# Queries and keys projected with rows on partitions, and brought to their stacks through a scratch array

## What is computed

```python
q = (target @ Wq.T + bq).reshape(B, L, H, D).transpose(0, 2, 1, 3)
k = (context @ Wk.T + bk).reshape(B, K, H, D).transpose(0, 2, 1, 3)
v = (context @ Wv.T + bv).reshape(B, K, H, D).transpose(0, 2, 1, 3)
q = _apply_rope(q, cos_q, sin_q)          # x * cos + _rotate_half(x) * sin
k = _apply_rope(k, cos_k, sin_k)
attn = jnp.einsum('bhld,bhkd->bhlk', q, k) * scale
attn = jnp.where(context_mask[:, None, None, :], attn, -jnp.inf)
attn = jax.nn.softmax(attn, axis=-1)
x = jnp.einsum('bhlk,bhkd->bhld', attn, v)
```

## Time and profile before

| | us |
|---|---|
| median of 3 runs | 795.33 |
| lowest, highest | 793.04, 796.99 |
| the profiled execution | 795.87 |
| its span | 794.0 |

### The profile page before, as it was taken

The page is one execution under the profiler, slowest core; times in us unless marked ns, Lnnn a source line. Parts: engine busy times, 40 slices in busy tenths (PEclk is TensorE's granted clock), DMA queues, the critical chain, the costliest instruction groups (busy, mean ns, idle before and its releaser), DMA issues. The chain is left out here.

```text
span 794.0 us, 10607 instructions
## 1 busy us (share of the span) xinstructions
PE 689.2 (87%) x3503; PEld 441.0 (56%) x3522; DVE 473.1 (60%) x852; ACT 358.8 (45%) x644; POOL 283.2 (36%) x462
## 2 busy tenths in 40 slices
PE   3599959999999996878999999995699999966986
PEld 1277733433344333745777777774376776852554
DVE  3567658888888841746834343434355546447985
ACT  0156644888888886345432222431313031102665
POOL 1446523344433450580001010101040436246897
PEclk9799986999999999989999999998789899986999
DMA  6000000000000004800100000001100000000001
GB/s 195 14 27 26 20 8 0 1 1 1 1 1 1 1 1 164 314 15 0 70 37 1 1 0 0 1 0 43 25 1 0 1 1 0 1 0 2 26 33 47
DMA packets 14103, 21.43 MB, mean 27 GB/s; under 512 B 2161, under 2 KB 11505, under 8 KB 13297
## 3 DMA queue, kind: packets, MB, share of 16 engines
q1 hardware_dynamic: 13200, 20.34, 7.5%
q10 hardware_dynamic: 864, 0.59, 0.3%
HBM read 18.83 MB, written 2.10 MB: 26 GB/s over the span
## 5 line engine op out<-in xcount | busy, mean ns | idle before, releaser
L562 DVE TENSOR_REDUCE mx<-ps_f 128x2 f32<-128x1024 f32 x128 | 151.5, 1220 | 31.6 <-PE ps_f L500 31.3
L638 ACT ACTIVATE prob<-ps_s 128x512 f32<-128x512 f32 x256 | 134.6, 608 | 34.5 <-PE ps_s L518 34.5
L518 PE MATMUL ps_s<-q_stacks,k_stacks 64*128 64x512 f32 x256 | 90.2, 484 | 5.9 <-ACT prob L638 3.5
L518 PEld LDWEIGHTS ps_s<-q_stacks,k_stacks 64*128 64x128 f32 x256 | 35.8, 188 | 87.2 <-ACT prob L638 70.9
L500 PE MATMUL ps_f<-k_stacks,q_stacks 64*128 64x512 f32 x256 | 63.8, 449 | 6.8 <-DVE mx L562 5.3
L527 PE MATMUL ps_o<-prob,vst 128*32 128x512 f32 x512 | 69.0, 612 | 0.0
L1018 ACT ACTIVATE qs<-ps_g 128x512 f32<-128x512 f32 x40 | 23.9, 598 | 88.6 <-PE ps_u L902 88.6
L1085 DVE SCALAR_TENSOR_TENSOR h<-ps_u,most,qs 128x512 f32<-128x512 f32 x32 | 24.0, 751 | 62.5 <-ACT qs L1018 62.5
L589 POOL TENSOR_TENSOR q_stacks<-minus,q_stacks 128x1024 fp32r<-128x1024 f32 x16 | 38.0, 2372 | 55.0 <-ACT minus L629 55.0
L172 POOL TENSOR_TENSOR norm_tmp_att<-st 128x4 f32<-128x4 f32 x4 | 1.0, 240 | 142.4 <-DVE st L1124 142.4
L1527 ACT ACTIVATE qs<-ps_SC,nmax 128x512 f32<-128x512 f32 x16 | 11.0, 686 | 76.4 <-DVE nmax L1415 76.4
(11 more groups left out here) (278 smaller groups left out, 1524.2 us busy)
## 6 DMA issues: line engine op xcount, KB each, us to landing
up<-in_up SPq DMA_DIRECT2D x10, 256.0 KB, 6.7
x<-in_x SPq DMA_DIRECT2D x4, 512.0 KB, 8.0
ctxT<-in_ctxT SPq DMA_DIRECT2D x16, 128.0 KB, 2.1
ks<-in_ctxTC SPq DMA_DIRECT2D x1, 2048.0 KB, 13.3
ks<-in_ctx SPq DMA_DIRECT2D x1, 2048.0 KB, 18.8
out<-x SPq DMA_DIRECT2D x16, 128.0 KB, 1.7
down<-in_down SPq DMA_DIRECT2D x1, 1280.0 KB, 5.5
ks<-in_wqv SPq DMA_DIRECT2D x1, 1024.0 KB, 20.7
```

The source lines that it names most:

```text
L518: pe.matmul(ps_s[n % 3][:, :], ks[rows(h), 2 * s + pair, kt * P:(kt + 1) * P], qs[rows(h), 2 * s + pair, :], start=True, stop=True).then_i ...
L562: dve.tensor_reduce(mx[:, f % 2, qt, 2 * pair:2 * pair + 2], ps_f[n % 2][:, :, :], AX_X, ALU.max).then_inc(used, 1)
L638: act.activation(prob[:, kt % 2, j, :], ps_s[n % 3][:, :], ACT.Exp, scale=SCALE)\
```

## The change

Per batch instead of per tile, queries and keys are projected with their rows on the partitions (two products of 128 output rows by 512 columns). The rows are ordered so that the two halves of a head lie in the two 128-row halves, and the rotation is then four products with a cosine and a sine table by VectorE (`turn_parts`, L341 and L344) and two sums by GpSimd (`add_parts`, L441 and L442). ScalarE rounds the high part (L414). High and low parts are written as they lie to an array in device memory (`room_k`, `room_q`), and are read back with the pattern of the stacks, 16 rows a transfer. For batch 0 SP reads them as plain 32-bit words into a landing place (where batch 2's stacks will be), from which ScalarE and VectorE copy them, rounding, into the stacks. For batches 1 to 3 GpSimd issues the reads, which cast to fp32r on the way: batch 1's keys at the end of prepare, its queries at the start of attend, and those of batches 2 and 3 in steps 1, 2, 4 and 5 of attend. The rows for maxima and mask come by DMA too, and a query's unused rows are cleared. The stack transposes and their copies go. TensorE waits before units 32, 64 and 96 for a batch's landing, and uses 53 rows of a head's 64 (`USED`).

The core of the diff:

```diff
+            def load_ctx(b):
+                if b > 1:
+                    sp.wait_ge(k_done, b - 1)
+                    sp.wait_ge(v_done, QT * (b - 1))
+                sp.dma_start(ctx_raw[:, b % 2, :, :], a["ctxTC"][:, :, b * S:(b + 1) * S]).then_inc(ctx_in[b % 2], 16)
...
+            for b in range(B):
+                sp.wait_ge(high_done, 2 * b + 1)
+                stacks.write(sp, "k", b, 0, k_out)
+                sp.wait_ge(k_low, b + 1)
+                stacks.write(sp, "k", b, 1, k_out)
+                if b + 2 < B:
+                    load_ctx(b + 2)
+                if b == 0:
+                    sp.wait_ge(k_out, 32)
+                    stacks.first_read(sp, "k")
+                sp.wait_ge(high_done, 2 * b + 2)
+                stacks.write(sp, "q", b, 0, turned["q_out"])
+                sp.wait_ge(q_low, b + 1)
+                stacks.write(sp, "q", b, 1, turned["q_out"])
+                if b == 0:
+                    sp.wait_ge(turned["q_out"], 32)
+                    sp.wait_ge(turned["landed"][0], FIRST_K)
+                    stacks.first_read(sp, "q")
+            sp.wait_ge(k_out, 32 * B)
...
+            for b in range(B):
+                if b:
+                    keys(b)
+                transposes(b)
+                values(b)
+                queries(b)
...
+            def turn_parts(b, which):
+
+                done, held, out = ((k_done, ps_k, k_out), (q_done, ps_q, turned["q_out"]))[which]
+                n = 2 * b + which
+                dve.wait_ge(done, b + 1)
+                wait(dve, out, 32 * b)
+                wait(dve, summed, n)
+                for c in range(DC):
+                    dve.scalar_tensor_tensor(out=part[which][:, c, :], in0=held[c][:, :], scalar=bqk[:, which, c:c + 1],
+                                             in1=trig[:, 0, :], op0=ALU.add, op1=ALU.mult)
+                for c in range(DC):
+                    last = dve.scalar_tensor_tensor(out=turn[:, 1 - c, :], in0=held[c][:, :],
+                                                    scalar=bqk[:, which, c:c + 1], in1=trig[:, 1, :], op0=ALU.add,
+                                                    op1=ALU.mult)
+                last.then_inc(parts, 1)
...
+            for b in range(B):
...
+                turn_parts(b, OF_K)
...
+                if b + 1 < B:
...
+                    ln_vector(dve, b + 1, (QT * (b + 1), QT * (b + 2)))
+                copy_values(b)
+                low_k(b)
+                turn_parts(b, OF_Q)
+                if b == B - 2:
+                    dve.wait_ge(turned["landed"][0], FIRST_K + FIRST_Q)
+                    for half in range(2):
+                        own = slice(4 * half, 4 * half + 4)
+                        dve.tensor_copy(qs[:, own, :], stacks.landing["q"][:, own, :])
...
+            for b in range(B):
+                transposed(b)
+                if b == B - 2:
+                    act.wait_ge(turned["landed"][0], FIRST_K)
+                    for half in range(2):
+                        own = slice(4 * half, 4 * half + 4)
+                        act.copy(ks[:, own, :], stacks.landing["k"][:, own, :])
+                high_part(b, OF_K)
+                if b + 1 < B:
+                    normalise(b + 1)
+                high_part(b, OF_Q)
...
+            def add_parts(b, which):
+                pool.wait_ge(parts, 2 * b + which + 1)
+                pool.tensor_tensor(part[which][:, 0, :], part[which][:, 0, :], turn[:, 0, :], ALU.subtract)
+                pool.tensor_tensor(part[which][:, 1, :], part[which][:, 1, :], turn[:, 1, :], ALU.add).then_inc(summed, 1)
...
+            def low_q(b):
+                pool.wait_ge(high_done, 2 * b + 2)
+                pool.tensor_tensor(low[OF_Q][:, :, :], part[OF_Q][:, :, :], high[OF_Q][:, :, :].bitcast(F32), ALU.subtract)\
+                    .then_inc(q_low, 1)
+            for n in "qk":
+                pool.memset(stacks.landing[n][:, :, :], 0.0).then_inc(preset, 1)
             ln_pool(pool, 0, (0, QT))
-            pool.wait_ge(consts, 16 * 2)
...
+            stacks.clear_queries(pool, 1)
+            for b in range(B):
+                add_parts(b, OF_K)
+                if b:
+                    low_q(b - 1)
+                if b + 1 < B:
+                    ln_pool(pool, b + 1, (QT * (b + 1), QT * (b + 2)))
+                if b == B - 1:
+                    pool.wait_ge(k_out, 32 * 2)
+                    pool.wait_ge(mask_done, 2)
+                    stacks.read_keys(pool, 1)
+                add_parts(b, OF_Q)
+            low_q(B - 1)
...
+    def places(self, to, name, b):
+        for h in range(2):
+            for o, part in enumerate((0, 0, 1) if name == "q" else (0, 1, 0)):
+                at = ROWS * h + HD * o
+                src = self.a["room_" + name][b, part].rearrange("(s a i) c n -> a (i c) s n", a=2, s=H // 2)[h]
+                yield to[at:at + HD, :, :], src
...
+    def write(self, sp, name, b, part, out):
+        src = self.turned["low" if part else "high"][name == "q"]
+        sp.dma_start(self.a["room_" + name][b, part], src[:, :, :].bitcast(F32)).then_inc(out, 16)
+
+    def read_keys(self, pool, b):
+        own = self.to["k"][:, 8 * b:8 * b + 8, :]
+        for dst, src in self.places(own, "k", b):
+            pool.dma_start(dst, src).then_inc(self.landed[b], 16)
...
+            dst, src = self.fixed(own, "k", h)
+            pool.dma_start(dst, src).then_inc(self.landed[b], 16)
+            at = ROWS * h + MASK_ROW
+            pool.dma_start(own[at:at + 1, :, :], self.mask_source(b)).then_inc(self.landed[b], 16)
...
+    def clear_queries(self, pool, b):
+        pool.memset(self.to["q"][:, 8 * b:8 * b + 8, :].bitcast(F32), 0.0).then_inc(self.turned["cleared"], 1)
+
+    def read_queries(self, pool, b):
+        own = self.to["q"][:, 8 * b:8 * b + 8, :]
+        pool.wait_ge(self.turned["cleared"], b)
+        for dst, src in self.places(own, "q", b):
+            pool.dma_start(dst, src).then_inc(self.landed[b], 16)
+        for h in range(2):
+            dst, src = self.fixed(own, "q", h)
+            pool.dma_start(dst, src).then_inc(self.landed[b], 16)
...
+PER_BATCH = 16 * (6 + 2 + 2 + 6 + 2)
...
+                if n % (UNITS * NG) == 0 and n:
+                    pe.wait_ge(turned["landed"][f // NG], PER_BATCH)
...
+            def stacks_ahead(s):
+
+                if s == 0:
+                    pool.wait_ge(turned["q_out"], 32 * B)
+                if s in (1, 4):
+                    stacks.read_keys(pool, 2 + s // 4)
+                    stacks.clear_queries(pool, 2 + s // 4)
+                if s in (2, 5):
+                    stacks.read_queries(pool, 2 + s // 4)
+            pool.wait_ge(turned["q_out"], 32 * 2)
+            stacks.read_queries(pool, 1)
...
             for s in range(STEPS):
+                stacks_ahead(s)
                 if s > 1:```

`load_ctx` reads the context of one batch whole. The line numbers of the change that the text names are those of the changed file.

GpSimd's queue at the end of the prepare stage, before; `qkb` are the projected rows with bias, `qkr` and `rope` the rotation's parts:

```order
L393 TENSOR_TENSOR qkr<-qkb,c 128x512
L395 TENSOR_TENSOR rope<-qkb,c 128x32x8
L397 TENSOR_TENSOR rope<-qkb,c 128x32x8
L207 UNCONDITIONAL_BRANCH
L565 UNCONDITIONAL_BRANCH
L567 MEMSET mt 128x1024
```

More of the change, by code:

```diff
@@ L54 @@
 MAX_ROW, MASK_ROW = 3 * HD, 3 * HD + 4
+USED = MASK_ROW + 1
 UNITS, LEAD = 2 * QT, 14
@@ L218, in phase_prepare @@
[L218 to L226, removed]
@@ L236, in phase_prepare @@
+        k_out = turned["k_out"]
+        turned["spent"] = [parts, summed, high_done, k_low, q_low, q_done, v_done, v_copied, k_done, xT_done]
         block = ctx.enter_context(nc.Block())
         va_v = va[:, :, :].rearrange("p s (k j d) -> p s k j d", k=QT, j=G)
-        slots = lambda u, side: stack[:, u, side, :, :].rearrange("p h (o d) -> p h o d", d=HD)
         @block.sync
@@ new lines, in low_k, with copy_values @@
+            def low_k(b):
+                dve.wait_ge(high_done, 2 * b + 1)
+                dve.tensor_tensor(low[OF_K][:, :, :], part[OF_K][:, :, :], high[OF_K][:, :, :].bitcast(F32), ALU.subtract)\
+                   .then_inc(k_low, 1)
+            def copy_values(b):
+                for q in range(QT):
+                    n = QT * b + q
+                    dve.wait_ge(v_done, QT * b + 2 * (q // 2) + 2)
+                    out = va_v[:, b * NG:(b + 1) * NG, q:q + 1, :, 0:HD].rearrange("p g k j d -> p (g k) j d")
+                    heads = lambda v: v.rearrange("p (g j d) -> p g j d", g=NG, j=G)
+                    dve.tensor_tensor(out, heads(ps_v[q // 2][:, q % 2, :]), heads(bv[:, :]), ALU.add)\
+                       .then_inc(v_copied, 1)
@@ new lines, in transposed, with high_part @@
+            def transposed(b):
+                act.wait_ge(xT_done, b + 1)
+                wait(act, q_done, b)
+                act.copy(xnT[:, :, :], ps_T[:, :, :]).then_inc(xT_copied, 1)
```

(7 more changed lines are left out.)

362 lines of the change are left out of this document (166 added, 196 removed).

## The result

The change made the kernel slower: 806.44 us (median of 4 runs, 804.50 to 808.48) against 795.45 (4 runs, 793.04 to 796.99), ratio 1.0147 with a 95% interval of 1.0127 to 1.0167. That is +11.0 us; the forecast was +19.8. The profiled span is 805.9 us against 794.0, so the traces differ by 11.9.

The account below looks back on a forecast made before the run. TensorE was taken to bound attend, the queries' buffer loop the changed prepare stage. Prepare -11.2, attend's start +1.2, waits +25.8 and clock +4.0 sum to +19.8 us on 795.87: 815.7; forecast's own range 806 to 840, whole range 783 to 842.

Parts of the forecast that it names:

- The price of a GpSimd issue: Time one DMA issue holds GpSimd: taken as 1.03 us, with 0.46 and 1.27 as ends of the range.
- steps 1 and 4: Attend: ten issues and a 3.8 us memset, 14.1 us against 4.9 free, delay TensorE by 9.2 us each.
- steps 2 and 5: Attend: eight issues, 8.2 us against 4.5 free on GpSimd, delay TensorE by 3.7 us each.
- the waits: Attend: TensorE waits for maxima behind GpSimd's issues and memset, twice (9.2 + 3.7), 25.8 us in all.
- The clock: Attend: long stalls cool TensorE; 2.0 us added for each of two stalls of 9 us, +4.0.
- The prepare stage: Stage before attend, 109.2 us before the change: forecast to end at 98, giving -11.2 us.
- its loop: Prepare: products overwrite the queries' buffer only after the previous batch's low part has landed; 16.5 us, taken as 18.2.
- SP standing at its waits for the first reads: Prepare: with hand-overs, lengthens the loop from 16.5 to 18.2 us a round.
- the ten issues: Prepare, last batch: GpSimd's DMA issues before the last queries' sums, from about 77 to 87.3 us at 1.03 each.
- their landing costs nothing: Attend: reads for batches 1 to 3 are issued steps ahead, so landing costs nothing unless 11 us are not enough.
- Cheap issues: Rival, chance 0.30: a GpSimd issue takes 0.46 us, attend pays 7.0, prepare ends about 94.3; 788 us.
- the scratch trip is slow: Rival, chance 0.10: 512 KB writes land in 6 us, not 3.2; prepare ends at 107 or later; 825 us.

Follow-up runs that it names:

- wide: The changed kernel with batch 0's twelve SP reads landing on 128 partitions each instead of 16, same bytes, output not the reference's; 797.60 us.
- the combined kernel: The changed kernel with batch 0's query reads after batch 1's key writes, batch 1's key reads in attend's step 0, and the edits of spread; 775.18 us.
- end_read: The combined kernel with one of batch 1's ten key reads moved to the end of GpSimd's program in the prepare stage; 782.19 us (one run).
- spread: The changed kernel with values staged first and GpSimd's reads for batches 2 and 3 laid six a step over attend's steps 2 to 4 and 6 to 8; 794.83 us.

## Why the prediction was right in sign, and where its steps failed

**The price of a GpSimd issue** was taken as 1.03 us from ScalarE's repeated-row load and measured 0.52 to 0.63, near the lower end of 0.46. With 0.55 my own working gives 5.5 + 3.8 - 4.9 = 4.4 us of waiting for steps 1 and 4 and nothing for steps 2 and 5. In wide, where the clock had risen before step 1 began, TensorE's wait there is just that:

```profile
134.61 1.11 PE L597 MATMUL ps_s<-c,mt 128*128 128x128 f32 x4 [3.98 <-POOL mt L670]
```

In the change itself it waited only 2.3 us, as the step began 3.2 us at the low clock and TensorE came later to the maxima. That its step 1 grew by 4.3, near the 4.4, is chance: 2.3 are the wait, 2.0 the clock. The mechanism of the wait was right and its term mis-sized: the waits cost 7.2 us, where 25.8 stood. I had argued that the shape of a transfer costs issue time. It doesn't here: six reads onto 16 partitions, eight onto 128 and one of 16 KB all held GpSimd 0.53 to 0.58 us an issue. The rule of the Trainium skill that I set against my price (page "DMA: Bandwidth & Descriptors", section "Anatomy of one DMA — SWDGE (gpsimd) path": generation is a small share of 2 us) sides with what was measured rather than with my price.

**The clock** stood in the sum with 4.0 us and measured 5.5. Behind the waits in steps 1 and 4 it was 0.50 for 3.2 and 5.9 us of work, at half speed an estimated 1.6 and 2.9, against the 2.0 each that I added. I had it for two stalls of 9 us; waits of 2.3 and 5.1 were enough. **Steps 2 and 5** should by the price cost nothing and cost 1.1 and 0.8: TensorE waited no longer in them than before, and its work took just that much more. The low clock left over from the start of attend, 3.2 us of step 1, is an estimated 1.6 more, which I had at nothing (the three estimates come to a little more than the 5.5 measured). **Step 4** cost 2.2 us over step 1, by the wait for staged values, which I had missed though the prediction names the value copy as queued behind the issues.

**The prepare stage** was forecast at 98 and ended at 108.3. The order of its loop was right, and in the combined kernel, where the keys' writes land in about 3.5 us, it ends at 88. Three steps failed. The first: "SP standing at its waits for the first reads" was given part of 1.7 us, but batch 1's key writes, ready at 36.4 and 40.8, were issued at 48.3 and 48.8 and then landed in up to 14.3 us, since the engines were full with slow reads ahead of them. The rounds between the queries' products were 21.1, 28.3 and 17.9 us against 18.2 taken; only the last is the loop that I described. The second: the ten issues stood in the sum with GpSimd's time alone; their landing had no term ("their landing costs nothing" I wrote of the reads in attend only, and there it held). The landing held the end of the stage by some 6.8 us (GpSimd's idle time there is 7.6 with the ten reads and 0.8 without). The third: I excluded full DMA engines with the 7% of the earlier trace rows, which says nothing of the transfers that the change itself adds.

**The rivals.** "Cheap issues" and "the scratch trip is slow" were kept apart, each with the other term as forecast. Both happened. Cheap issues gave 788, and a stage that ends at 108.3 rather than 94.3 adds 14: 802, where 806.4 was measured; what steps 2, 4 and 5 took beyond that case (4.1 us) is most of the rest. So the sign was right by luck: two errors of opposite sign, 18 us too much in attend and 10 too little in the stage, met halfway, and the kernel was 1.4% slower at a price at which I had forecast faster. That 806.4 still lies in the 806 to 840 of the forecast, at its very edge, is luck of the same kind. "Wrong: a prepare stage of 105 us or more, with VectorE waiting" was the line that came true, for keys rather than for queries.

**Right as forecast:** queries of batch 0 ready at 24.6 (25.7 taken), TensorE and VectorE no longer the bound of the stage, TensorE's wait for mt in step 1, no unit of attend waiting for a landing, no change behind attend (485.7 us against 485.9).

## What to carry to other kernels

Before a queue is given new transfers, ask three things of each: what is issued behind it and wanted soon, onto how many partitions it lands, and whether a stage ends before it has landed. Work that an engine with idle time takes over is free only in pieces smaller than the room of one step: 18 issues a batch in two lumps cost 12.7 us over two batches, in three sixes nothing that could be measured. And a wait costs more than its length, if the clock falls behind it. And if two uncertain terms pull in opposite ways, price the case in which both are wrong.

## What the hardware showed beyond the expectation

- While reads onto 16 partitions were under way, the DMA engines were full (share 1.05 to 1.61) at 111 to 115 GB/s; with as many bytes onto 128 partitions, and other transfers among them, windows with a share of 0.88 to 1.08 moved 282 to 326. By which limit isn't told apart here.
- A DMA issue held GpSimd 0.52 to 0.63 us, for 16 KB as for 256 KB, and 0.85 us where it stood alone (end_read).
- GpSimd's end of stage waited for the landing of its own DMAs (5.4 us for one read, 13.1 to 13.4 for the last of ten); SP's did not.
- After a wait of TensorE of 2.3 us the granted clock was 0.50 for 3.2 us, after one of 5.1 for 5.9, while TensorE was busy throughout.
- Beside VectorE's two rounding copies of 128x2048 a GpSimd sum took 3.32 us instead of 1.27 (3.31 in spread and in the combined kernel):

```profile
76.56 2.35 DVE L391 CAST q_stacks<-q_landing 128x2048 fp32r<-128x2048 f32 x2
...
76.71 3.32 POOL L441 TENSOR_TENSOR q_part<-q_part,turn 128x512 f32<-128x512 f32 x1 [4.08 <-DVE turn L344]
```
